# Turning a feed-forward down projection: sign matrix held still, gelu's output moved, two batches a turn

## The chip, the cores and the metric

One core of one Trainium2 chip runs the whole program. The metric is device microseconds of one execution; the kernel before takes 2285.94 us (median of three runs, 2284.62 to 2286.42). PE is the matrix engine, DVE the vector engine, ACT the scalar engine, POOL the GpSimd engine, SP the engine that issues most DMAs.

## The reference

Six blocks follow one another on x of 32 batches of 256 tokens of 128 channels: a feed-forward block with binarised weights, a gated attention unit, the same feed-forward block again, a mixture of experts, a linear attention, the mixture of experts again. The change lies in the feed-forward block, which runs twice:

```python
def _binarize(w):
    alpha = mean(abs(w), axis=1, keepdims=True)
    return alpha * sign(w)
h = gelu(x @ bw1.T + b1)          # 128 channels to 512
out = h @ bw2.T + b2              # 512 to 128: the down projection
x = x + 0.5 * out                 # _L0_ffn_ref(_layernorm(x))
```

Row d of bw2 is a single number alpha[d] times a row of signs, and d is the output's channel.

## The kernel before

x stays in SBUF as 66 tiles of 128 tokens by 128 channels. The six blocks are stages with a barrier between: ffn0, gau1, ffn2, moe3, lin4, moe5, after a short setup. Within a stage every engine has its own program, a fixed order of instructions, and semaphores (`Signal`) join them. `ffn_stage` (line 526) is written for both runs: `first` marks ffn0, `route` marks ffn2.

A turn of the stage is one batch, two tiles. DVE normalises (L262 into `xn`), PE transposes (L690) to bank 4, ACT writes the high part in float32r (L742) and DVE the low part (L605): `parts` holds x as a sum of two float32r numbers. PE's `up` multiplies w1's signs with both parts, 4 chunks of 128 hidden units, eight matmuls of 256 columns (L699). ACT applies gelu to each chunk (L749) into `hT`. PE's `down` (L709) takes `hT` as the stationary operand and `w2T`, the binarised w2 in float32, as the moving one: 2 tiles x 4 chunks = 8 float32 matmuls of 128 columns, each two records in the trace. Tokens come out on partitions, so DVE adds half of them to x (L611), adds the bias (L617 in ffn0; POOL does it ahead in ffn2, L580) and takes the statistics for the next stage's norm (L274).

PE's order in a turn is up(b+1), transpose(b+3), down(b). Beside it, DVE does small pieces of norm work: in ffn0 the statistics of the second half of x, two tiles a batch over sixteen batches, and `norm.piece` (moments, then three Newton steps) for these and for the next stage. POOL computes the position bias of gau1 in ffn0 (`group_bias`, 32 buckets), and a difference of weights.

ffn2 also routes the first four batches of moe3 ahead (`RouteAhead`), by `TURNS_AHEAD` (line 1634): batch n of four begins at batch turn 7 + 5n, and each of its steps stands a number of turns later: norm 0, split 1, choose 2, mask 3, assign 4, first 5 (POOL compares slot numbers, L382, called hot below), hot0 6 and hot1 7 (DVE adds the second choice, L523, and waits for POOL's), sends 8 and 9 (PE, L425).

## Time and profile before

| | us |
|---|---|
| median of three runs | 2285.94 |
| the profiled execution | 2280.57 |
| its span | 2278.7 |
| PE busy in the span | 2170.7 (95%) |
| DVE busy | 1522.8 (67%) |
| ACT busy | 1242.7 (55%) |
| POOL busy | 690.7 (30%) |

Busy time counts an engine's instructions, not its waits. PE's matmuls are pipelined and their ends are modelled, so the spacing of two starts tells more than a duration. The two feed-forward stages are about a tenth of the span.

### The profile page before, as it was taken

The numbers are of one execution on the slowest core, as the hardware profiler recorded it, in microseconds if no ns is written. First come the engines' busy times: TensorE is split into PE (matmuls) and PEld (weight loads), VectorE is DVE, ScalarE is ACT, GpSimd is POOL, SyncE is SP. The second block draws the span as 40 slices with busy tenths as digits, with TensorE's granted clock in tenths as the row PEclk, the third lists the DMA queues.
The fourth block names the chain that finished last, engine by engine and source line by source line (L and its number), as shares of the span: only waits on it lengthen the run. The fifth ranks groups of instructions, "written<-read, shape, count | busy, mean of one in ns | idle before, by whom it ended". The sixth has DMA issues, their size and how long they took to land. (4 is left out here: it accounts for less than half of the span.)

```text
span 2278.7 us, 42519 instructions
## 1 busy us (share of the span) xinstructions
PE 2170.7 (95%) x13706; PEld 1748.3 (77%) x13706; DVE 1522.8 (67%) x4922; ACT 1242.7 (55%) x2504; POOL 690.7 (30%) x724
## 2 busy tenths in 40 slices
PE   5989998999999999899999999999999899999995
PEld 5978888977777777777777777877777777777775
DVE  6867776876777776556565566666666666777664
ACT  4645445754554554465566665666665444545542
POOL 0412222533575655500000000000100344665545
PEclk9999999999999999999999999999999999999998
DMA  8040000000111111200000000000000011111122
GB/s 276 0 176 0 0 0 1 2 10 22 36 41 43 37 38 44 56 7 0 0 0 0 0 0 1 1 1 1 1 1 1 12 28 40 46 51 49 51 55 73
DMA packets 70648, 68.44 MB, mean 30 GB/s; under 512 B 9312, under 2 KB 57952, under 8 KB 70112
## 3 DMA queue, kind: packets, MB, share of 16 engines
q1 hardware_dynamic: 60960, 47.62, 6.6%
q0 software_dynamic: 8192, 16.79, 3.2%
q10 hardware_dynamic: 1344, 2.16, 0.4%
q8 instruction: 76, 1.25, 0.2%
q14 instruction: 76, 0.62, 0.1%
HBM read 32.47 MB, written 34.08 MB: 29 GB/s over the span
## 5 line engine op out<-in xcount | busy, mean ns | idle before, releaser
L2034 ACT ACTIVATE moe_fc<-moe_bank,all_b_fc 128x380 f32<-128x380 f32 (+2 forms) x448 | 245.8, 549 | 277.7 <-PE moe_bank L1964 274.6
L2141 DVE SCALAR_TENSOR_TENSOR moe_act<-moe_bank,all_b_moe_gate,moe_fc 128x380 f32<-128x380 f32 (+2 forms) x448 | 256.7, 576 | 168.3 <-PE moe_bank L1968 101.4
L1980 PEld LDWEIGHTS moe_bank<-all_w_proj,moe_act 128*128 128x128 f32 x2560 | 300.0, 192 | 12.2 <-issue 2.4
L1980 PE MATMUL moe_bank<-all_w_proj,moe_act 128*128 128x128 f32 x2560 | 305.7, 276 | 2.0 <-DVE moe_expert_out L2150 2.0
L1803 POOL DMA_INDIRECT all_landed<-rows_out,all_take_at x256 | 271.7, 1061 | 117.9 <-issue 113.4
L1494 POOL COPY lin_xn_ones<-lin_xn 128x254 f32<-128x254 f32 x32 | 12.7, 398 | 720.7 <-PE lin_bank L1244 720.4
L2041 ACT ACTIVATE moe_act<-moe_act 128x760 f32<-128x760 f32 (+2 forms) x224 | 174.7, 780 | 93.2 <-DVE moe_act L2141 92.7
L1879 POOL TENSOR_SCALAR moe_hot<-all_slot_ids,moe_slot 128x608 fp32r<-128x608 f32 x112 | 203.3, 1824 | 68.3 <-DVE moe_slot L2118 33.7
L1388 ACT ACTIVATE lin_neg<-lin_bank 128x512 f32<-128x512 f32 x256 | 151.7, 592 | 105.5 <-PE lin_bank L1236 61.9
L1286 PEld LDWEIGHTS lin_bank<-lin_kv,lin_qT 128*128 128x128 f32 x1024 | 145.0, 192 | 74.4 <-issue 62.3
L1964 PE MATMUL moe_bank<-gau_rowsT,all_w_fc 128*128 128x380 f32 (+2 forms) x448 | 170.1, 461 | 1.6 <-ACTq L2045 1.6
L1968 PE MATMUL moe_bank<-gau_rowsT,all_w_gate 128*128 128x380 f32 (+2 forms) x448 | 167.6, 456 | 0.8 <-DVE moe_act L2141 0.8
L1392 ACT ACTIVATE lin_neg<-lin_neg 128x512 f32<-128x512 f32 x256 | 161.1, 630 | 7.9
L1416 ACT ACTIVATE lin_gate_tanh<-lin_bank,all_bg_half 128x256 f32<-128x256 f32 x256 | 103.5, 468 | 108.3 <-PE lin_bank L1263 108.2
L1286 PE MATMUL lin_bank<-lin_kv,lin_qT 128*128 128x130 f32 x1024 | 153.5, 277 | 9.1 <-DVE lin_heads L1541 8.7
L749 ACT ACTIVATE ffn_hT<-ffn_bank,all_b,all_alpha 128x256 f32<-128x256 f32 x248 | 119.8, 564 | 57.9 <-PE ffn_bank L699 57.9
L1964 PE MATMUL moe_bank<-moe_rowsT,all_w_fc 128*128 128x380 f32 (+1 forms) x384 | 148.0, 467 | 0.0
L1968 PE MATMUL moe_bank<-moe_rowsT,all_w_gate 128*128 128x380 f32 (+1 forms) x384 | 145.9, 462 | 0.0
L1236 PE MATMUL lin_bank<-all_wk,lin_xT 128*128 128x512 f32 x256 | 131.2, 617 | 2.9 <-ACT lin_xT L1384 1.7
L1556 DVE TENSOR_TENSOR all_x<-lin_bank,all_x 128x256 f32<-128x256 f32 (+1 forms) x32 | 13.6, 425 | 177.2 <-PE lin_bank L1310 177.2
L1310 PE MATMUL lin_bank<-all_wo,lin_gated 128*128 128x128 f32 x1024 | 127.8, 278 | 0.8 <-DVE lin_gated L1550 0.8
L709 PE MATMUL ffn_bank<-all_w2T,ffn_hT 128*128 128x128 f32 x1024 | 125.9, 276 | 1.9 <-DVE all_x L611 1.9
(248 smaller groups left out, 4472.8 us busy)
## 6 DMA issues: line engine op xcount, KB each, us to landing
rows_out<-moe_expert_out SPq DMA_DIRECT2D x96, 128.0 KB
rows_out<-all_zeros SPq DMA_DIRECT2D x1, 9728.0 KB, 28.7
rows_out<-moe_expert_out SPq DMA_DIRECT2D x80, 62.0 KB
all_landed<-rows_out,all_take_at POOLq DMA_INDIRECT x256, 2.7
out<-all_x SPq DMA_DIRECT2D x5, 640.0 KB, 4.5
all_w_fc<-in_w_fc SPq DMA_DIRECT2D x1, 2048.0 KB, 9.8
all_w_gate<-in_w_gate SPq DMA_DIRECT2D x1, 2048.0 KB, 13.6
all_w_proj<-in_w_proj SPq DMA_DIRECT2D x1, 2048.0 KB, 18.1
```

What stands on the lines that cost most here:

```text
L1236: nc.tensor.matmul(bank[j][:, :], xT[:, j // 2 * P:(j // 2 + 1) * P], k.wk[:, j % 2 * HU:(j % 2 + 1) * HU], start=True, stop=True).then_in ...
L1286: last = nc.tensor.matmul(bank[4 + n % 2][:, i * 2 * DH1:(i + 1) * 2 * DH1], qT[:, p, t * P:(t + 1) * P], kv[:, p, :], start=True, stop=True)
L1388: nc.scalar.activation(neg[:, j, :], bank[place][:, :], ACT.Relu, scale=-1.0).then_inc(negs.sem, 1)
L1392: nc.scalar.activation(neg[:, j, :], neg[:, j, :], ACT.Exp, scale=-1.0).then_inc(exps.sem, 1)
L1803: nc.gpsimd.indirect_dma_start(landed[:, b % LANDED, t, h, :], None, k.rows_out, bass.IndirectOffsetOnAxis(take_at[:, i, h:h + 1], 0), bou ...
L1879: nc.gpsimd.tensor_scalar(hot[:, b % 2, t, :], k.slot_ids[:, :], slot[:, b % 2, t, 0:1], None, ALU.is_equal).then_inc(hot_first, 1)
L1964: nc.tensor.matmul(bank[FC + j % 2][:, 0:c.width], k.w_fc[:, e, j * P:(j + 1) * P], rows[c.n][:, e, 0:c.width], start=True, stop=True).the ...
L1968: nc.tensor.matmul(bank[GATE + j % 2][:, 0:c.width], k.w_gate[:, e, j * P:(j + 1) * P], rows[c.n][:, e, 0:c.width], start=True, stop=True) ...
L1980: last = nc.tensor.matmul(bank[OUT][:, j * DIM:(j + 1) * DIM], act_in[:, i % 2, h, j * P:(j + 1) * P], k.w_proj[:, e * MC + h, :], start=( ...
L2034: nc.scalar.activation(fc[:, j, 0:c.width], bank[FC + j % 2][:, 0:c.width], ACT.Identity, bias=k.b_fc[:, e * MC + j:e * MC + j + 1]).then_ ...
L2041: nc.scalar.activation(a, a, ACT.Silu).then_inc(act_sb, 1)
L2141: nc.vector.scalar_tensor_tensor(act_in[:, i % 2, j, 0:c.width], bank[GATE + j % 2][:, 0:c.width], k.b_moe_gate[:, e * MC + j:e * MC + j + ...
```

## The change

The down projection is turned: w2's signs are the stationary operand and gelu's output is the moving one, so the output has channels on partitions. There alpha[d] is a factor per partition. ACT applies it with the bias (`out_columns`, Identity with scale 0.5 alpha and bias 0.5 b2) on the way out of PSUM to `outT`; PE transposes that back into the same bank (`back`), and DVE adds it to x (`add_out`).

A turn is two batches, 512 columns. Of the four chunks of hidden units, two (`SPLIT`) are multiplied in float32r, as a high part, cast by POOL (`gelu_high`), and a low part, subtracted by DVE (`gelu_low`); the other two in float32 (`w2_whole`, `h_whole`). POOL also normalises the second of the two batches. The bias additions of DVE and POOL go. The position bias on POOL is cut into pieces that follow the casts and normalisations of turns 5 to 15; in ffn0 the statistics of x's second half are four tiles per batch turn, at batch turns 0 to 3 and 8 to 11, the norm pieces for them at 4 to 7 and 12 to 15. The routing begins at batch turn 8 instead of 7, and `rowsT` is split in two tensors. The hardware loops of ffn0 are written out.

```diff
-                link(nc.vector.scalar_tensor_tensor(dif[:, 1, :], sgn[:, 1, :], alpha[:, FC:], w2[:, 0, :], ALU.mult, ALU.subtract))
-                nc.vector.tensor_copy(bin_w[:, 0, :], sgn[:, 0, :]).then_inc(bin_ready, 1)
-                nc.vector.tensor_tensor(bin_w[:, 1, :], w2[:, 0, :], dif[:, 1, :], ALU.add).then_inc(bin_ready, 1)
+                for i in range(2):
+                    nc.vector.tensor_copy(bin_w[:, i, :], sgn[:, i, :]).then_inc(bin_ready, 1)
+                nc.vector.tensor_scalar(k.out_scale[:, :], alpha[:, FC:], 0.5, None, ALU.mult).then_inc(prepared, 1)
...
+DUO = 2
+SPLIT = 2
+ON_SCALAR = 0
+TURNS = BATCHES // DUO
+DT = DUO * TILES
+DS = DUO * SEQ
...
+        h_whole = k.sb("h_whole", [P, 2, FC - SPLIT, DS])
+        h_high_of = k.sb("h_high", [P, 2, SPLIT, DS], F32R)
+        h_low_of = k.sb("h_low", [P, SPLIT, DS], F32R)
+        outT = k.zeros if route else k.sb("outT", [P, DS])
...
+                def normalise(p):
+                    pool.wait_ge(xn_ready.sem, xn_ready.at(p))
+                    for t in range(TILES, DT):
+                        last = norm.apply(xn[:, t, :], 0, 0, p * DT + t, engine=nc.gpsimd)
+                    last.then_inc(half_xn.sem, 1)
+                def gelu_high(p):
+                    for c in range(ON_SCALAR, SPLIT):
+                        pool.wait_ge(h_sb.sem, h_sb.at(p, 0, c))
+                        nc.gpsimd.tensor_copy(h_high_of[:, p % 2, c, :], hT[:, c, :]).then_inc(h_high.sem, 1)
+                for p in range(3):
+                    normalise(p)
+                gelu_high(0)
+                for p in range(TURNS):
+                    if p + 1 < TURNS:
+                        gelu_high(p + 1)
+                    if p + 3 < TURNS:
+                        normalise(p + 3)
+                    if first and p >= 5:
+                        group_bias.add(pool, BUCKETS * (p - 5) // (TURNS - 5), BUCKETS * (p - 4) // (TURNS - 5))
+                    if route:
+                        for s in range(DUO):
+                            routing.on_gpsimd(pool, DUO * p + s)
...
+                def low_part(p):
+                    dve.wait_ge(high_sb.sem, high_sb.at(p))
+                    nc.vector.tensor_tensor(parts[:, p % 2, 1, :], bank[ROWS_T][:, :], parts[:, p % 2, 0, :], ALU.subtract).then_inc(xT_sb.sem, 1)
+                def gelu_low(p):
+                    if p:
+                        dve.wait_ge(o_ps.sem, o_ps.at(p - 1))
+                    for c in range(SPLIT):
+                        if c < ON_SCALAR:
+                            dve.wait_ge(h_high_act.sem, h_high_act.at(p))
+                        else:
+                            dve.wait_ge(h_high.sem, h_high.at(p, 0, c - ON_SCALAR))
+                        nc.vector.tensor_tensor(h_low_of[:, c, :], hT[:, c, :], h_high_of[:, p % 2, c, :], ALU.subtract).then_inc(h_low.sem, 1)
+                def add_out(p):
+                    dve.wait_ge(back_ps.sem, back_ps.at(p))
+                    nc.vector.tensor_tensor(rows(p), rows(p), bank[OUT][:, :].rearrange("p (t d) -> p t d", t=DT),
+                                            ALU.add).then_inc(summed.sem, 1)
...
+                def own_norm(b):
+                    if first:
+                        if b < 4 or 8 <= b < 12:
+                            part = b // 8
+                            if b % 8 == 0:
+                                dve.wait_ge(k.x_in[KNOWN + part], 16)
+                            for t in range(2 * TILES):
+                                i = X_PART * (KNOWN + part) + 2 * TILES * (b % 8) + t
+                                last = nc.vector.bn_stats(k.stats[:, i, :], k.x[:, i, :])
+                            if b % 8 == 3:
+                                last.then_inc(late, 1)
+                                dve.wait_ge(late, 2 + part)
+                        elif b < 16:
+                            part, piece = b // 8, b % 8 - 4
+                            lo = X_PART * (KNOWN + part)
+                            norm.piece(dve, chain, lo, X_TILES if part else lo + X_PART, piece)
+                    elif b < PIECES:
+                        norm.piece(dve, chain, AHEAD, X_TILES, b)
...
+                    gelu_low(p)
+                    if p:
+                        add_out(p - 1)
+                    if p + 3 < TURNS:
+                        normalise(p + 3)
+                    if p + 2 < TURNS:
+                        low_part(p + 2)
+                    beside(DUO * p)
+                    if p:
+                        stats(p - 1)
+                    beside(DUO * p + 1)
...
-                def down(b, par):
-                    pe.wait_ge(summed.sem, summed.at(b, -1, 0))
-                    for i in range(2):
-                        pe.wait_ge(h_sb.sem, h_sb.at(b, 0, i))
-                    for t in range(TILES):
-                        for c in range(FC):
-                            last = nc.tensor.matmul(bank[5][:, t * DIM:(t + 1) * DIM], hT[:, par, c, t * P:(t + 1) * P],
-                                                    k.w2T[:, c, :], start=(c == 0), stop=(c == FC - 1))
+                def down(p):
+                    pe.wait_ge(h_sb.sem, h_sb.at(p))
+                    if p:
+                        pe.wait_ge(summed.sem, summed.at(p - 1))
+                    for c in range(SPLIT, FC):
+                        nc.tensor.matmul(bank[OUT][:, :], k.w2_whole[:, c - SPLIT, :], h_whole[:, p % 2, c - SPLIT, :], start=(c == SPLIT), stop=False)
+                    for c in range(SPLIT):
+                        pe.wait_ge(h_low.sem, h_low.at(p, 0, c))
+                        nc.tensor.matmul(bank[OUT][:, :], k.w2T[:, c, :], h_high_of[:, p % 2, c, :], start=False, stop=False)
+                        last = nc.tensor.matmul(bank[OUT][:, :], k.w2T[:, c, :], h_low_of[:, c, :], start=False, stop=(c == SPLIT - 1))
                     last.then_inc(o_ps.sem, 1)
...
+                def back(p):
+                    pe.wait_ge(o_sb.sem, o_sb.at(p))
+                    for t in range(DT):
+                        last = nc.tensor.transpose(bank[OUT][:, t * P:(t + 1) * P], outT[:, t * P:(t + 1) * P], k.ident[:, :])
+                    last.then_inc(back_ps.sem, 1)
...
+                for p in range(TURNS):
+                    if p + 2 < TURNS:
+                        transpose(p + 2)
+                    if p + 1 < TURNS:
+                        up(p + 1, range(2))
+                    if p:
+                        back(p - 1)
+                    if p + 1 < TURNS:
+                        up(p + 1, range(2, FC))
...
+                def out_columns(p):
+                    act.wait_ge(o_ps.sem, o_ps.at(p))
+                    nc.scalar.activation(outT[:, :], bank[OUT][:, :], ACT.Identity, bias=k.b2_half[:, 0:1],
+                                         scale=k.out_scale[:, 0:1]).then_inc(o_sb.sem, 1)
```

PE in ffn2, before: one batch's turn from up to down, and what stands around it (L396 and L402 are the routing's).

```order
L709 MATMUL ffn_bank<-all_w2T,ffn_hT 128x128 x8
L396 MATMUL ffn_bank<-all_ident,ffn_route_xn 128x128 x2
L699 MATMUL ffn_bank<-ffn_x_parts,all_w_signT 128x256 x8
L690 MATMUL ffn_bank<-all_ident,ffn_xn 128x128 x2
L709 MATMUL ffn_bank<-all_w2T,ffn_hT 128x128 x8
L402 MATMUL ffn_bank<-all_w_router,ffn_route_xT 128x8 x2
```

A batch has ten matmuls in up and transpose and eight in down. Now, PE in ffn0, one turn of two batches.

```order
L748 MATMUL ffn_bank<-all_ident,ffn_xn 128x128 x4
L757 MATMUL ffn_bank<-ffn_x_parts,all_w_signT 128x512 x4
L776 MATMUL ffn_bank<-all_ident,ffn_outT 128x128 x4
L757 MATMUL ffn_bank<-ffn_x_parts,all_w_signT 128x512 x4
L766 MATMUL ffn_bank<-ffn_h_whole,all_w_sign_wholeT 128x512 x2
L769 MATMUL ffn_bank<-ffn_h_high,all_w_signT 128x512
L770 MATMUL ffn_bank<-ffn_h_low,all_w_signT 128x512
L769 MATMUL ffn_bank<-ffn_h_high,all_w_signT 128x512
L770 MATMUL ffn_bank<-ffn_h_low,all_w_signT 128x512
```

The two batches' sixteen float32 matmuls of 128 columns have become two of 512 in float32 and four of 512 in float32r, and four transposes (`back`) stand between the halves of up.

POOL in ffn2, around the routing's second batch, before.

```order
L580 TENSOR_TENSOR all_x<-all_x,all_b_half 128x256
L372 CAST ffn_route_parts<-ffn_route_xn 128x256
L374 TENSOR_TENSOR ffn_route_parts<-ffn_route_xn,ffn_route_parts 128x256
L580 TENSOR_TENSOR all_x<-all_x,all_b_half 128x256 x4
L382 TENSOR_SCALAR ffn_route_hot<-all_slot_ids,ffn_route_slot 128x608 x2
```

Between two hots stand bias additions and one split. Now, the same place.

```order
L616 CAST ffn_h_high<-ffn_hT 128x512 x2
L262 TENSOR_SCALAR ffn_xn<-all_x,all_mean,all_rstd 128x128 x2
L616 CAST ffn_h_high<-ffn_hT 128x512 x2
L262 TENSOR_SCALAR ffn_xn<-all_x,all_mean,all_rstd 128x128 x2
L390 TENSOR_SCALAR ffn_route_hot<-all_slot_ids,ffn_route_slot 128x608 x2
L380 CAST ffn_route_parts<-ffn_route_xn 128x256
L382 TENSOR_TENSOR ffn_route_parts<-ffn_route_xn,ffn_route_parts 128x256
```

The hot now stands behind a turn's two casts and two normalisations, and in the same turn of two batches as the split after it.

DVE in ffn2, the same batch, as it is now.

```order
L262 TENSOR_SCALAR ffn_route_xn<-all_x,all_mean,all_rstd 128x128 x2
L668 BN_STATS all_stats<-all_x 128x6 x4
L531 SCALAR_TENSOR_TENSOR ffn_route_hot<-all_slot_ids,ffn_route_slot,ffn_route_hot 128x608
L658 TENSOR_TENSOR ffn_h_low<-ffn_hT,ffn_h_high 128x512 x2
L662 TENSOR_TENSOR all_x<-all_x,ffn_bank 128x512
L262 TENSOR_SCALAR ffn_xn<-all_x,all_mean,all_rstd 128x128 x2
```

DVE's hot0 (L531), which waits for POOL's hot, stands in front of the next turn's gelu_low and add_out.

## Rows read from the trace of the kernel before

**Rows 1.** Busy time by stretch: length, PE, PEld, DVE, ACT, POOL, clock, DMA share, GB/s.

```profile
22.00:132.00 110.00, 99.73 (x832) 96.92 (x832) 88.49 (x312) 71.74 (x161) 26.75 (x71) 1.00 0.26 99
364.00:477.00 113.00, 106.68 (x904) 104.85 (x904) 87.13 (x327) 75.59 (x174) 44.05 (x49) 0.97 0.01 2
```

**Rows 2.** Timeline, first and last of ffn0 and ffn2: start us, us, engine, line.

```profile
22.84 0.60 DVE L262 TENSOR_SCALAR ffn_xn<-all_x,all_mean,all_rstd 128x128 f32<-128x128 f32 x2 [1.22 <-PEq L684]
26.02 2.06 PE L699 MATMUL ffn_bank<-ffn_x_parts,all_w_signT 128*128 128x256 f32 x8
131.46 0.11 DVE L678 TENSOR_SCALAR all_bg_half<-all_bg 128x8 f32<-128x8 f32 x1
364.49 0.60 DVE L262 TENSOR_SCALAR ffn_xn<-all_x,all_mean,all_rstd 128x128 f32<-128x128 f32 x2 [0.81 <-PEq L684]
475.56 0.49 DVE L274 BATCH_NORM_STATS2 all_stats<-all_x 128x6 f32<-128x128 f32 x2
```

**Rows 3.** Timeline of one batch's turn in ffn0.

```profile
102.73 1.20 PE L699 MATMUL ffn_bank<-ffn_x_parts,all_w_signT 128*128 128x256 f32 x8
103.50 1.93 ACT L749 ACTIVATE ffn_hT<-ffn_bank,all_b,all_alpha 128x256 f32<-128x256 f32 x4 [0.77 <-PE ffn_bank L699]
103.77 0.38 PE L690 MATMUL ffn_bank<-all_ident,ffn_xn 128*128 128x128 f32 x2
103.99 1.95 PE L709 MATMUL ffn_bank<-all_w2T,ffn_hT 128*128 128x128 f32 x16
104.01 0.49 DVE L274 BATCH_NORM_STATS2 all_stats<-all_x 128x6 f32<-128x128 f32 x2
105.69 1.20 PE L699 MATMUL ffn_bank<-ffn_x_parts,all_w_signT 128*128 128x256 f32 x8
```

**Rows 4.** Timeline of PE in lin4 (float32) and ffn2 (L425, float32r).

```profile
421.49 0.81 PE L425 MATMUL ffn_bank<-ffn_route_hot,ffn_route_parts 128*128 128x304 f32 x4
422.13 1.11 PE L699 MATMUL ffn_bank<-ffn_x_parts,all_w_signT 128*128 128x256 f32 x8
...
1414.91 1.02 PE L1236 MATMUL lin_bank<-all_wk,lin_xT 128*128 128x512 f32 x2
1415.77 0.50 PE L1286 MATMUL lin_bank<-lin_kv,lin_qT 128*128 128x130 f32 x3
```

**Rows 5.** Groups by line and form: busy us, mean ns, idle before.

```profile
L1528 DVE SCALAR_TENSOR_TENSOR lin_qT<-lin_bank,lin_neg 128x512 f32<-128x512 f32 x128 | 85.3, 687 | 9.2 <-ACT lin_neg L1392 6.8
L1041 POOL TENSOR_SCALAR gau_relu<-gau_sim 128x256 f32<-128x256 f32 x32 | 27.0, 844 | 221.0 <-DVE gau_sim L1103 221.0
L1871 POOL CAST moe_parts<-moe_xn 128x256 fp32r<-128x256 f32 x56 | 22.3, 398 | 249.8 <-DVE moe_xn L262 164.8 <-issue 85.1
L292 POOL TENSOR_SCALAR all_pos_bias<-all_bias_sum 32x32 f32<-32x32 f32 x4 | 1.2, 292 | 0.3
L302 POOL COPY all_wv_less_last_row<-all_ident 128x16 f32<-128x16 f32 x1 | 0.2, 201 | 0.0
```

**Rows 6.** Timeline of ffn0: POOL's position bias, DVE's moments (first and last).

```profile
55.58 0.41 POOL L284 TENSOR_SCALAR all_bias_one<-all_buckets,all_rel 128x32 f32<-128x32 f32 x1
...
84.00 1.40 POOL L292 TENSOR_SCALAR all_pos_bias<-all_bias_sum 32x32 f32<-32x32 f32 x4
84.23 0.17 DVE L227 TENSOR_TENSOR all_mean<-all_stats 128x18 f32<-128x18 f32 x1
...
85.48 0.18 DVE L236 TENSOR_SCALAR all_rstd<-all_var 128x18 uint32<-128x18 uint32 x1
```

**Rows 7.** Timeline, two places where DVE's normalisations meet a POOL instruction.

```profile
85.48 2.39 POOL L300 TENSOR_TENSOR all_wv_less_last_row<-all_wv,ffn_wv_last_row 128x1024 f32<-128x1024 f32 x1
85.69 2.52 DVE L262 TENSOR_SCALAR ffn_xn<-all_x,all_mean,all_rstd 128x128 f32<-128x128 f32 x2
...
410.95 1.05 DVE L262 TENSOR_SCALAR ffn_xn<-all_x,all_mean,all_rstd 128x128 f32<-128x128 f32 x2
411.15 3.73 POOL L382 TENSOR_SCALAR ffn_route_hot<-all_slot_ids,ffn_route_slot 128x608 fp32r<-128x608 f32 x2 [2.17 <-DVE ffn_route_slot L516]
```

More of the change, by code:

```diff
@@ L636, in _, with beside @@
+                def beside(b):
+                    own_norm(b)
+                    next_norm(b)
+                    if route:
+                        routing.read_psum(dve, b)
+                        routing.on_vector(dve, b)
+                for p in range(2):
+                    normalise(p)
+                    low_part(p)
+                normalise(2)
                 if first:
@@ L730, in _ @@
+                if route:
+                    for b in range(BATCHES, routing.last_turn() + 1):
                         routing.on_tensor(pe, b)
+                back(TURNS - 1)
             @block.scalar
             def _(act):
-                act.sem_inc(h_sb.sem, h_sb.credit)
                 if first:
                     act.wait_ge(k.b_in, 32)
-                def high_part(b, lag, par):
-                    act.wait_ge(xT_ps.sem, xT_ps.at(b, lag))
-                    if not (isinstance(b, int) and lag < 2):
-                        act.wait_ge(h_ps.sem, h_ps.at(b, lag - 2))
-                    nc.scalar.copy(parts[:, par, 0, :], bank[4][:, 0:SEQ]).then_inc(high_sb.sem, 1)
@@ L744, in gelu @@
-                def gelu(b, lag, par):
-                    act.wait_ge(o_ps.sem, o_ps.at(b, lag - 2))
-                    for i in range(2):
-                        act.wait_ge(h_ps.sem, h_ps.at(b, lag, i))
-                        for c in (2 * i, 2 * i + 1):
-                            last = nc.scalar.activation(hT[:, par, c, :], bank[2 * par + i][:, (c % 2) * SEQ:(c % 2 + 1) * SEQ],
-                                                        ACT.Gelu, bias=k.b1[:, c:c + 1], scale=k.alpha[:, c:c + 1])
-                        last.then_inc(h_sb.sem, 1)
@@ L753, in _ @@
-                for b in range(2):
-                    high_part(0, b, b % 2)
-                for i in range(2):
-                    act.wait_ge(h_ps.sem, h_ps.at(0, 0, i))
-                    for c in (2 * i, 2 * i + 1):
-                        last = nc.scalar.activation(hT[:, 0, c, :], bank[i][:, (c % 2) * SEQ:(c % 2 + 1) * SEQ],
-                                                    ACT.Gelu, bias=k.b1[:, c:c + 1], scale=k.alpha[:, c:c + 1])
-                    last.then_inc(h_sb.sem, 1)
@@ new lines, in gelu @@
+                def gelu(p):
+                    if p >= 2:
+                        act.wait_ge(o_ps.sem, o_ps.at(p - 2))
+                    for c in range(FC):
+                        act.wait_ge(h_ps.sem, h_ps.at(p, 0, c))
+                        if p and c < SPLIT:
+                            act.wait_ge(h_low.sem, h_low.at(p - 1, 0, c))
+                        nc.scalar.activation(hT[:, c, :] if c < SPLIT else h_whole[:, p % 2, c - SPLIT, :], bank[c][:, :], ACT.Gelu,
+                                             bias=k.b1[:, c:c + 1], scale=k.alpha[:, c:c + 1]).then_inc(h_sb.sem, 1)
+                    if ON_SCALAR:
+                        act.wait_ge(h_sb.sem, h_sb.at(p, 0, 0))
+                        nc.scalar.copy(h_high_of[:, p % 2, 0, :], hT[:, 0, :]).then_inc(h_high_act.sem, 1)
@@ L774, in _ @@
+                for p in range(TURNS):
+                    if p:
+                        out_columns(p - 1)
+                    if p + 2 < TURNS:
+                        high_part(p + 2)
+                    if route:
+                        routing.on_scalar(act, DUO * p)
+                    if p + 1 < TURNS:
+                        gelu(p + 1)
+                    if route:
+                        routing.on_scalar(act, DUO * p + 1)
+                out_columns(TURNS - 1)
                 if route:
```

276 lines of the change are left out of this document (113 added, 163 removed).

## The prediction

> **What bounds the kernel now.** I read the busy times by stretch first, then the timeline of one turn, then the two ends of the stages that the change touches. The profiled execution took 2280.57 us with a span of 2278.7. The two feed-forward stages, ffn0 and ffn2, are 22.84 to 131.57 and 364.49 to 476.05 [rows 2]: 108.7 and 111.6 us, together 220.3. In both, PE is busy for some 100 us and more, at full granted clock but for the start of the second [rows 1]. The reader is to see in the timeline of a turn [rows 3] that PE goes from one group to the next without a hole: eight up matmuls from 102.73, two transposes from 103.77, sixteen records of the down projection from 103.99, the next turn's up from 105.69. So one batch costs 2.96 us and PE sets it. In that turn ACT needs 1.93 us for four gelus, and DVE's instructions are 0.3 to 0.6 us each. POOL has in ffn0 only the position bias, which ends early [rows 6], and in ffn2 one addition a batch and the routing. So the change takes work from the engine that sets the turn, and gives work to two that had room; the question is whether that room lasts.
>
> **The steady turn of two batches.** Per pair PE now spends 2 x 2.96 = 5.92 us. Afterwards, by spacing, it has these to do. The transposes in: four at 0.11 (two took 103.77 to 103.99 [rows 3]) = 0.44; the transposes back, which are new, 0.44 as well. Up: eight float32r matmuls of 512 columns. No row has that width. Eight of 256 take 1.04, 0.13 each [rows 3], so 0.26 is the upper end; a float32 matmul of 512 columns takes 0.86 (1414.91 to 1415.77, two records [rows 4]), and a quarter, 0.215, is the lower. Four of 304 columns took 0.64 [rows 4], between. I take 0.23: 1.84. Down: two float32 matmuls of 512 at 0.86 = 1.72, and four float32r of 512 at 0.23 = 0.92. Before, a pair's down took 2 x 1.70 = 3.40.
>
> Sum 0.44 + 1.84 + 0.44 + 1.72 + 0.92 = 5.36. The chain beside it is as long: the end of down(p-1) reaches ACT in some 0.2, out_columns takes 0.7 (a gelu of 256 columns, also with scale and bias, takes 0.48 with its neighbours, a quarter of 1.93 [rows 3], so 0.5 to 0.97, and part of it is fixed), but back(p-1) stands behind 0.44 of transposes and 0.92 of up, so it starts at 1.36 without waiting and ends at 1.80; add_out (0.69 [rows 5]) ends near 2.75, and PE, through with the second half of up at 2.72, waits 0.05 for it. A turn is 5.41, 0.51 less than now, and sixteen turns give 8.2 a stage if nothing else is late.
>
> **Fill and drain.** The first turn is longer: a normalisation on DVE (0.6 [rows 2]), its other half on POOL (1.4, below), four cold transposes, the cast, low part, and all of it again for the second pair before PE may go to its up (it stands behind transpose(1)): 7.1. Eight cold ups, at double price as the first group of before shows (2.06 for eight, against 1.20 warm [rows 2, 3]), bring 10.8, the last gelu, cast and low part 13.4, and down 2.63: 16.0. Fifteen turns more, the last two at 5.1 since no up is left, make 96.6. The drain is serial: ACT 1.0, back 0.65, add 0.75, statistics 0.9, block end 0.4: 3.7. A stage with nothing in the way would take 100.3.
>
> **What stands in the way in ffn0.** DVE's ordinary turn: two gelu_low, add_out and low_part of 512 columns at 0.62 spacing (0.69 less the 0.07 by which neighbours overlap), two normalisations 0.52, four statistics at 0.205 (0.49 is two [rows 3]): 3.82. That fits in 5.41. But the statistics of x and the norm pieces, which stood spread over sixteen batches, now crowd into turns 0 to 7. Four turns get eight statistics more, 1.64. With some 0.4 of waits they are near 5.85: 4 x 0.45 = 1.8. Two get moments (eight instructions, 84.23 to 85.66 [rows 6], 1.5) and a Newton step (three such instructions, each waiting for the one before, 0.6), 5.9 and waits, 6.5: 2 x 1.1 = 2.2. Two get two Newton steps: 2 x 0.25 = 0.5.
>
> POOL's turn: two casts of 512 columns. 256 take 0.398 and 16 take 0.201 [rows 5], on that line 0.61 each. Two normalisations of 128 columns with two operations: no row; one operation takes 0.29 at 32 and 0.84 at 256 columns [rows 5], and those are my ends; 0.53 lies on their line, and I take 0.7, the nearer to 0.84, for the second operation. At 0.29 the stages would be some 6 us together shorter than I write, at 0.84 some 4 longer. That is 2.6. From turn 5 on it also has the position bias, 0.89 for each of 32 buckets (55.58 to 84.00 [rows 6]), so 2.9 a turn and 2.6 us: 5.2, with waits 5.75, over five turns that are not DVE's already: 5 x 0.35 = 1.8.
>
> Together 6.3: ffn0 takes 100.3 + 6.3 = 106.6, **2.1 less** than now.
>
> **What stands in the way in ffn2.** PE's routing work is the same instructions as before: 106.68 - 99.73 = 7.0 [rows 1], so 107.3. POOL loses the bias additions, but its routing hot, 3.73 for two [rows 7], now shares the queue with casts and normalisations. The order of batch turns 18 and 19, and 28 and 29, is what I look at: POOL's hot and DVE's hot0 fall in the same pair there, where a whole turn lay between them before. POOL comes to hot only after two casts (which start at 3.05 after the last down) and two normalisations, at 6.0; DVE is at hot0 at 6.5 and waits until 7.9, then for POOL's access, and the gelu_low, add_out and normalise behind it are late with PE's down behind them: 2.2, and 0.9 the last time, where little is queued. In the other routing turns POOL's casts start behind hot, or DVE's routing steps meet its fuller turn: 4 x 0.7 = 2.8. Norm pieces 1.2. Together 7.1, bounds 0 and 14: ffn2 takes 107.3 + 7.1 = 114.4, **2.8 more** than now.
>
> Other edits: setup loses one DVE instruction of 512 and has another ACT copy; DVE waits there for x anyway, so nothing. The position bias and the V weights move to POOL's end of ffn0, level with DVE's drain (2.4 for the largest [rows 7]); if POOL is later, up to 2 are lost. The stages after the two are the same instructions.
>
> **Sum.** -2.1 + 2.8 = +0.7. On the median of 2285.94 (5.4 above the profiled execution; I carry that difference over) it is 2286.6; I write 2287.
>
> **A rule weighed.** Casts and DVE's two-input subtractions want the same access. [rows 7] has both answers: a DVE normalisation issued 0.2 after a 2.39 us POOL subtraction ended only with it (2.52 for two, 0.60 free [rows 2]), but two issued around a 1.83 us POOL comparison took 1.05, so only 0.46 was lost. I therefore let a cast hold for most of its 0.61, a hot only for parts, some 0.5 at each end.
> The Trainium skill, page "SBUF — State Buffer", section "Who interferes with whom", says that DVE instructions in a two-port mode, or with two SBUF inputs against a reading POOL instruction, take the shared pair as an exclusive lock for the whole instruction. The subtraction agrees; the comparison does not.
>
> **Rivals.** First, PE's saving stays: the other engines' waits are absorbed: DVE and POOL sums alone (3.82 and 2.6) are far below 5.41, and only PE is at its limit in [rows 1]. Without waits for access ffn0 loses only the crowded turns, half of 6.3, and ffn2 some 1.8 of 7.1: about 220.3 - 103.5 - 109 = -8, 2278. Against: the waits that [rows 7] shows.
> Second, POOL is slower at the two-operation normalisation. If the second operation doubles it, 0.94 each instead of 0.7 (POOL's own end above is 0.84): 0.48 a turn. It decides once POOL's turn with bias is above 5.41, which it then is (2 x 0.61 + 2 x 0.94 + 2.6 = 5.7, and waits, over 6). ffn0 +4, ffn2 +4 (hot0 later still): 2295.
> Third, and slower for certain, POOL holds its access throughout, and DVE waits out each hot and each TENSOR_SCALAR whole: 1.8 rather than 0.5 at up to eight hots in ffn2, and 0.3 more at casts. The four turns with hot go from 6.6 to about 9 by that, +10 in ffn2 and +1.5 in ffn0: 2299, slower. It decides where a DVE instruction meets a hot at its beginning. For it: the subtraction of 2.39. Against: 0.46 behind 1.83.
> The Trainium skill's sentence above, of "SBUF — State Buffer", would give this time.
> Fourth, float32r at 512 columns is at its upper end, 0.26: twelve a turn, 0.36 more, in the half of the turns that PE sets: 16 x 0.36 = 6, 2293. Against it: a float32 record of 512 columns, twice the work a column, takes 0.43. For it: 304 columns took 0.16, as much a column as 0.27 for 512 [rows 4].
>
> **Chances and range.** Forecast (no change, its own range 2282 to 2291): 0.42. Rival 1: 0.22. Rival 2: 0.21. Rival 3: 0.1, rival 4: 0.05. A measurement of this kernel tells 0.2%, 4.6 us, from no change; so faster 0.22, same 0.42, slower 0.36. The range for 8 in 10 runs from rival 1's time to rival 3's with a little at each end: 2277 to 2301.
>
> **What would show it.** The first place is PE between two groups of up matmuls in ffn0's turns 9 to 13: 5.4 to 5.8 apart; 5.9 and more says rival 2. POOL's ffn_h_high cast should last 0.6 and its ffn_xn 0.55 to 0.85. In ffn2 DVE should idle before the hot0 of batch turns 19 and 29, released by POOL. PE's waits should name DVE's add_out (all_x) in crowded turns and ffn_xn of POOL before transposes. The stages should take about 107 and 114. Wrong would be: float32r at 512 columns at more than 0.27 (PE's turn then 5.9 and no gain at all), a turn below 5.3, or time that changes in a later stage.

## The result: 5.3 us slower, 0.2%

| | median us | runs | ratio to before, 95% |
|---|---|---|---|
| before | 2285.48 | 13 | |
| changed | 2290.78 (2286.47 to 2293.03) | 13 | 1.0022 [1.0015, 1.0030] |

The stated range holds the time; it lies 3.8 us above the forecast, and its 5.3 us over before are just outside the 4.6 that the forecast called no change. The two profiled executions are further apart than the medians, 2280.57 and 2288.08, since that of before is one of its shortest. By the first instruction of each stage (the changed kernel's rows answer to [rows 2]; the last stage runs to the end of the span):

```profile
22.18 0.60 DVE L262 TENSOR_SCALAR ffn_xn<-all_x,all_mean,all_rstd 128x128 f32<-128x128 f32 x2 [0.94 <-PEq L129]
133.88 0.60 DVE L262 TENSOR_SCALAR gau_z<-all_x,all_mean,all_rstd 128x128 f32<-128x128 f32 x2 [1.00 <-PEq L926]
361.52 0.60 DVE L262 TENSOR_SCALAR ffn_xn<-all_x,all_mean,all_rstd 128x128 f32<-128x128 f32 x2 [0.54 <-DVE all_stats L274]
479.18 0.21 ACT L2121 ACTIVATE moe_tanh_gap_ahead<-all_gap_ahead 128x8 f32<-128x8 f32 x1 [2.42 <-PEq L588]
```

| us | before | before, a second profile | changed |
|---|---|---|---|
| ffn0 | 109.7 | 109.3 | 111.7 |
| gau1 | 231.9 | 232.3 | 227.6 |
| ffn2 | 112.3 | 112.3 | 117.7 |
| moe3 | 479.4 | 479.6 | 481.3 |
| lin4 | 821.0 | 821.0 | 823.3 |
| moe5 | 501.5 | 502.6 | 502.4 |

The two stages cost 7.3 us more, and gau1, moe3 and lin4, whose instructions are the same, moved by -4.3, +1.9 and +2.2 (moe5 by +0.9 against the one profile of before and by -0.2 against the other). Inside a turn the profile looks much as forecast. The timeline of one turn of ffn0 after the change, which answers to [rows 3]:

```profile
99.10 0.66 PE L748 MATMUL ffn_bank<-all_ident,ffn_xn 128*128 128x128 f32 x4 [0.17 <-POOL ffn_xn L262]
99.51 1.17 PE L757 MATMUL ffn_bank<-ffn_x_parts,all_w_signT 128*128 128x512 f32 x4
100.52 0.60 PE L776 MATMUL ffn_bank<-all_ident,ffn_outT 128*128 128x128 f32 x4
100.88 1.19 PE L757 MATMUL ffn_bank<-ffn_x_parts,all_w_signT 128*128 128x512 f32 x4
101.99 1.96 PE L766 MATMUL ffn_bank<-ffn_h_whole,all_w_sign_wholeT 128*128 128x512 f32 x4
103.61 1.60 POOL L262 TENSOR_SCALAR ffn_xn<-all_x,all_mean,all_rstd 128x128 f32<-128x128 f32 x2
104.02 0.40 PE L770 MATMUL ffn_bank<-ffn_h_low,all_w_signT 128*128 128x512 f32 x1
104.26 0.39 PE L769 MATMUL ffn_bank<-ffn_h_high,all_w_signT 128*128 128x512 f32 x1
104.49 0.40 PE L770 MATMUL ffn_bank<-ffn_h_low,all_w_signT 128*128 128x512 f32 x1
105.27 0.66 PE L748 MATMUL ffn_bank<-all_ident,ffn_xn 128*128 128x128 f32 x4 [0.38 <-POOL ffn_xn L262]
```

float32r of 512 columns starts every 0.235 us (0.23 forecast), a turn that nothing delays takes 5.55, and here PE waits at its transposes for POOL's normalisation, as the prediction named it. The granted clock is another matter. Windows of the changed kernel (from and to, length, busy us of PE, PEld, DVE, ACT, POOL, then the clock as a share of full speed, DMA):

```profile
122.00:124.70 2.70, 0.96 (x7) 0.47 (x5) 2.42 (x5) 0.78 (x1) 2.24 (x6) 1.00 0.00 0
124.70:129.30 4.60, 4.53 (x8) 2.12 (x8) 3.08 (x13) 0.03 (x1) 3.92 (x9) 0.63 0.00 2
466.00:469.70 3.70, 0.94 (x6) 0.42 (x4) 3.63 (x7) 0.78 (x1) 1.92 (x2) 1.00 0.01 2
469.70:474.20 4.50, 4.46 (x9) 2.26 (x10) 3.21 (x14) 0.00 (x0) 0.00 (x0) 0.62 0.00 0
479.00:490.00 11.00, 9.43 (x36) 6.66 (x37) 4.76 (x21) 6.24 (x12) 1.79 (x4) 0.84 0.01 1
```

In the last turn PE has no up left. It is busy for 0.96 of 2.70 us (0.94 of 3.70 in ffn2), waiting for ACT's out_columns and then DVE's add_out, and the granted clock falls from 1.0 to 0.5 (2.4 to 1.2 GHz) behind that: the last down takes 4.4 us in both stages, where others take 2.7. The clock falls again at the start of the mixture of experts, where it was 1.0 before:

```profile
476.63:488.00 11.37, 9.43 (x42) 6.46 (x43) 6.21 (x28) 7.04 (x15) 2.41 (x6) 1.00 0.01 1
```

In gau1 the opposite happened. Windows of before, then of the changed kernel:

```profile
139.10:142.50 3.40, 1.48 (x10) 1.06 (x9) 2.01 (x8) 1.68 (x4) 1.47 (x2) 0.99 1.04 387
142.50:145.90 3.40, 3.40 (x9) 2.69 (x9) 1.54 (x5) 1.34 (x3) 0.00 (x0) 0.50 1.03 386
```

```profile
139.00:146.00 7.00, 5.08 (x29) 4.10 (x28) 4.70 (x14) 3.71 (x9) 1.47 (x2) 1.00 1.05 409
```

Before, the clock fell a second time, behind a stretch in which PE was busy for 1.48 of 3.40 us; after the change it didn't. Both kernels also have a fall at the stage's start, and after the change that one began earlier, at the end of ffn0. Together gau1 ran at 0.5 for 9.9 us before and for 4.9 after. At half the clock 5.0 us less are worth 2.5 (an estimate), most of the 2.8 that it gained in its first 30 us (the rest of the 4.3 builds up in small steps over its first 160 us, and stays unexplained).

Each timed run also has a mean granted clock. Its median is 0.984 over the changed kernel's 13 runs and 0.987 over the 94 runs of before beside the experiments. Among the runs of either kernel a clock lower by 0.001 goes with 0.9 to 1.7 us more, so 0.003 go with some 3 to 5 us (an estimate): most of the difference.

### The profile page after: what moved, and what is told of

Same layout as the page of the kernel before. It is cut to its first block and busy times, and to the rows that moved or that the text cites. A ratio compares the mean times of both kernels' runs of the same rounds, so it can differ in the third digit from the quotient of the medians.

```text
span 2286.2 us, 40200 instructions
## 1 busy us (share of the span) xinstructions
PE 2164.8 (95%) x12810; PEld 1678.4 (73%) x12810; DVE 1521.6 (67%) x4826; ACT 1234.1 (54%) x2377; POOL 768.1 (34%) x820
## 5 line engine op out<-in xcount | busy, mean ns | idle before, releaser
L1569 POOL COPY lin_xn_ones<-lin_xn 128x254 f32<-128x254 f32 x32 | 12.8, 401 | 722.9 <-PE lin_bank L1319 722.5
L2039 PE MATMUL moe_bank<-moe_rowsT,all_w_fc 128*128 128x380 f32 (+1 forms) x576 | 226.0, 474 | 0.0
L2043 PE MATMUL moe_bank<-moe_rowsT,all_w_gate 128*128 128x380 f32 (+1 forms) x576 | 222.9, 469 | 0.0
L2043 PEld LDWEIGHTS moe_bank<-moe_rowsT,all_w_gate 128*128 128x128 f32 x576 | 109.2, 190 | 66.7 <-DVE moe_act L2216 0.9
L2225 DVE TENSOR_TENSOR moe_expert_out<-moe_bank,all_b_proj 128x384 f32<-128x384 f32 (+1 forms) x112 | 60.0, 536 | 100.6 <-PE moe_bank L2055 99.2
L1338 PE MATMUL lin_bank<-lin_xT,all_wg 128*128 128x256 f32 x512 | 126.5, 380 | 0.3 <-DVE lin_qT L1603 0.3
L1330 PE MATMUL lin_bank<-lin_xT,all_wq 128*128 128x256 f32 x512 | 125.8, 379 | 0.0
```

The lines of the kernel that those rows point to most:

```text
L2039: nc.tensor.matmul(bank[FC + j % 2][:, 0:c.width], k.w_fc[:, e, j * P:(j + 1) * P], rows[c.n][:, e, 0:c.width], start=True, stop=True).the ...
L2043: nc.tensor.matmul(bank[GATE + j % 2][:, 0:c.width], k.w_gate[:, e, j * P:(j + 1) * P], rows[c.n][:, e, 0:c.width], start=True, stop=True) ...
```

## Experiments

All times are medians; the kernel before ran beside each (2284.4 to 2285.2).

**The kernel before once more.**

> The kernel before once more, for a second profile of it. Between the two profiles on hand the stages that the change doesn't touch also differ: the gated attention's stage takes 231.9 us before and 227.6 after, and everything from the mixture of experts on 1801.9 and 1807.0. Theory: both are what two executions differ by; this profile then shows the later stages at 1803 to 1808 and the attention's stage between 227 and 232. Rival: the change itself makes the later stages 5 us longer and the attention's 4 us shorter; then this one shows 1802 and 232 again.

2281.03 in its profiled run. The rival holds: moe3 and lin4 are 479.6 and 821.0 again, gau1 232.3. In all kernels made from the changed one lin4 took between 821.0 and 823.9, with the granted clock at its start low for a shorter or longer time. So what the change does to later stages, it does through where PE's clock happens to fall in them. The traces bear this out: in all fourteen profiles lin4 took 821.0 to 821.1 where the clock was at 0.5 for 10.2 us of it, 821.9 to 822.9 for 13.7 and 823.0 to 823.9 for 17.1; moe3 took 479.4 to 479.7 without a fall and 481.0 to 481.7 with one.

**The routing's second choice one batch turn later.**

```diff
-"first": 5, "hot0": 6, "hot1": 7, "send0": 8, "land0": 9, "send1": 9, "land1": 10}
+"first": 5, "hot0": 7, "hot1": 8, "send0": 9, "land0": 10, "send1": 10, "land1": 11}
```

> Only the routing's table is changed: DVE's second choice (hot0) and all behind it come one batch turn later, so that POOL's comparison and DVE's hot0 no longer fall in the same turn of two batches. Theory: the two waits of 1.7 us of DVE for POOL's hot, in turns 9 and 14, go; turn 9 (7.9 us from down to down) and the turn with the other come to some 6.5; the last send comes a little later: 2 to 3 us less, 2288. Rival: it is POOL's queue (casts and normalisations behind two hots of 3.6 to 4.1 us) and the held access that make these turns long, and not DVE's wait; then the turns keep their 7 to 8 us and the time is 2290 to 2292.

2292.75, 1.0028 [1.0019, 1.0037]: not faster. In the changed kernel the wait is there in turn 9 as predicted: POOL's hot, DVE's hot0 and PE's down behind DVE's addition. (In turn 14, where the expectation has it too, the trace shows no such wait of DVE.)

```profile
432.10 3.60 POOL L390 TENSOR_SCALAR ffn_route_hot<-all_slot_ids,ffn_route_slot 128x608 fp32r<-128x608 f32 x2
433.95 1.35 DVE L531 SCALAR_TENSOR_TENSOR ffn_route_hot<-all_slot_ids,ffn_route_slot,ffn_route_hot 128x608 fp32r<-128x608 f32 x1 [1.73 <-POOL ffn_route_hot L390]
437.45 1.96 PE L766 MATMUL ffn_bank<-ffn_h_whole,all_w_sign_wholeT 128*128 128x512 f32 x4 [1.73 <-DVE all_x L662]
```

With the later hot0 turn 9 takes 5.99 instead of 7.92 us and turn 14 5.31 instead of 6.34, but turn 10 takes 8.46 instead of 7.00 and turn 8 7.03 instead of 6.24:

```profile
437.75 1.73 POOL L616 CAST ffn_h_high<-ffn_hT 128x512 fp32r<-128x512 f32 x2
439.48 1.58 POOL L262 TENSOR_SCALAR ffn_xn<-all_x,all_mean,all_rstd 128x128 f32<-128x128 f32 x2
441.11 0.65 PE L748 MATMUL ffn_bank<-all_ident,ffn_xn 128*128 128x128 f32 x4 [2.04 <-POOL ffn_xn L262]
```

POOL's casts and normalisations stand behind two hots and a split, and PE's transposes behind those. Turns 7 to 14 take 53.4 us together instead of 54.1: most of the wait moved to the next queue, as the rival (POOL's queue) has it.

**30 of 32 buckets of the position bias left out.**

```diff
-if first and p >= 5:
-    group_bias.add(pool, BUCKETS * (p - 5) // (TURNS - 5), BUCKETS * (p - 4) // (TURNS - 5))
+if first and p in (5, TURNS - 1):
+    group_bias.add(pool, p // (TURNS - 1), p // (TURNS - 1) + 1)
```

> 30 of the 32 buckets of the position bias are left out (so the attention's bias is not the reference's), which takes 2.6 us of POOL's time out of each of ffn0's turns 5 to 15. Theory: POOL's queue sets ffn0's turns 8 to 12 (30.2 us from down to down for the five, instead of 27.0 at PE's 5.4), since PE's transposes wait for POOL's half of the normalisations: the five come to 27.0 to 28.0 and the stage loses 2.5 to 3 us: 2288. Rival: DVE, with its waits, is as late as POOL, or PE sets the turn anyway; then the five keep some 29.5 to 30 and the time stays within 0.7 us.

2290.76, no change. But ffn0's turns 8 to 12 are 5.58, 5.58, 5.55, 5.55, 5.58: 27.8 us together instead of 30.2, as the theory said. Most of it was given back in the last turn:

```profile
119.90 2.35 POOL L308 TENSOR_TENSOR all_wv_less_last_row<-all_wv,ffn_wv_last_row 128x1024 f32<-128x1024 f32 x1
119.93 3.48 DVE L658 TENSOR_TENSOR ffn_h_low<-ffn_hT,ffn_h_high 128x512 fp32r<-128x512 f32 x2
124.15 3.46 PE L766 MATMUL ffn_bank<-ffn_h_whole,all_w_sign_wholeT 128*128 128x512 f32 x4 [2.79 <-DVE all_x L662]
```

POOL, earlier now, comes to the weights difference while DVE has the last gelu_low to do (3.48 us for two, 1.29 free), PE waits 2.79, and its four records take 3.46 instead of 1.96, at the low clock.

**No normalisation on POOL.**

```diff
-                    if p + 3 < TURNS:
-                        normalise(p + 3)
...
-                    for t in range(TILES):
+                    for t in range(DT):
                         last = norm.apply(xn[:, t, :], 0, 0, p * DT + t)
```

> POOL's half of the normalisations goes to DVE, in both stages and all turns: POOL has 1.6 us a turn less, DVE 0.52 more. Theory: POOL's queue makes the long turns (hots of 3.6 to 4.1 with casts and normalisations behind them, for which PE's transposes and DVE's subtractions wait; the bias in ffn0's turns 8 to 12): the four long turns of ffn2 come from 7.0 to 7.9 down to some 6.3, 4 to 5 us together, ffn0's turns 8 to 12 from 30.2 to 28, and the fill is 1.5 shorter in each stage; against it DVE's crowded turns 0 to 6 of ffn0 are 0.5 longer each: 2282 to 2286. Rival: it is DVE that is late in those turns, by its own load and by waiting for POOL's access behind the hot; then the long turns stay or grow by 0.5 each: 2290 to 2295.

2288.74, 1.0017 [1.0008, 1.0026], not told apart from the changed kernel's 1.0022; 2282 to 2286 had been expected. The long turns 7, 9 and 12 of ffn2 are 6.97, 7.02 and 6.84 (7.66, 7.92 and 7.29), but turn 10 is 8.24 (7.00), at full clock; there PE idles for 1.22 us and its sends start 0.1 behind the end of an addition of the second choice on DVE (441.47 to 442.30). The four long turns lost 0.8 us together, not 4 to 5. The fills are 2.0 and 3.6 us shorter, ffn0's turns 8 to 12 5.55 to 5.58; but its turns 1 to 7 are 6.0 to 6.9 (they were 5.6 to 6.6), and ffn2's turns 0 to 3 went from 5.5 to 5.6 up to 5.9 to 6.3, with PE behind DVE:

```profile
392.92 1.71 DVE L262 TENSOR_SCALAR ffn_xn<-all_x,all_mean,all_rstd 128x128 f32<-128x128 f32 x4
393.14 1.95 PE L753 MATMUL ffn_bank<-ffn_h_whole,all_w_sign_wholeT 128*128 128x512 f32 x4 [0.68 <-DVE all_x L650]
```

So POOL bounds the turns with a hot or the bias, DVE the others as soon as it gets more.

**The last down in a bank of its own.** The transposes' bank is free by then.

```diff
+        def out(p):
+            return bank[OUT if p < TURNS - 1 else ROWS_T]
...
-                    if p:
+                    if 0 < p < TURNS - 1:
                         pe.wait_ge(summed.sem, summed.at(p - 1))
...
+                    if p == TURNS - 1:
+                        back(p - 1)
```

> Only the last turn of both feed-forward stages is changed: its down projection goes to the PSUM bank of the transposes, which is free by then, so it waits neither for the addition of the turn before nor for its transposes back. Theory: in the changed kernel PE stands idle for some 2 us in the last turn, its granted clock then falls to 0.5 for 3.4 us and the last down takes 4.5 instead of 2.7 us; without the hole the clock stays at 1.0 there, the last down ends some 4 us earlier in ffn0 and 3 to 4 in ffn2 (where the routing's last sends then set the end): 2283 to 2285 us. Rival: the clock falls at the end of the stage whatever PE does; then only the hole of some 2 us a stage goes, and the drop shows in the last down all the same: 2287 to 2288.

2289.05, 1.0016 [1.0007, 1.0025]: 3.8 us over before instead of 5.3, with overlapping intervals, and above what theory and rival had (2283 to 2288). Over the last down the clock stays at 1.0, as the theory said, and it ends 3.7 us earlier. ffn0 isn't shorter all the same:

```profile
126.38 0.66 PE L782 MATMUL ffn_bank<-all_ident,ffn_outT 128*128 128x128 f32 x4 [0.87 <-ACT ffn_outT L833]
127.81 2.35 POOL L308 TENSOR_TENSOR all_wv_less_last_row<-all_wv,ffn_wv_last_row 128x1024 f32<-128x1024 f32 x1
127.87 2.42 DVE L242 SCALAR_TENSOR_TENSOR all_norm_tmp<-all_rstd 128x112 f32<-128x112 f32 x1
130.94 0.69 DVE L666 TENSOR_TENSOR all_x<-all_x,ffn_bank 128x512 f32<-128x512 f32 x1
```

The last transposes are done at 127.0; the addition comes at 130.94, behind a Newton step that waits out POOL's difference (2.42 us, 0.27 at its fellows). PE then stands idle for longer, and gau1 takes 230.7 instead of 227.6, at 0.5 of the clock for 11.4 us instead of 4.9. ffn2 with nothing of the kind is 3.3 us shorter (114.35).

**The same, and the weights difference in turn 4.** Its call at the end goes.

```diff
+                    if first and p == 4:
+                        weights_less_last_row(k, pool, last_row, wv1_done)
```

> The last down into its own bank, as in the run with only the last turn changed, and POOL's weights difference (2.35 us) in ffn0's turn 4 instead of at the end. Theory: in that run the last down of ffn0 ended 4 us earlier, but DVE's last Newton step stood behind POOL's difference (2.42 us instead of 0.28), with the last addition to x behind it, so that the stage was as long as before; with the difference gone from there ffn0 is 2 to 2.4 us shorter (111.7 to 109.4) and PE's hole in front of the attention is shorter by as much: 2285 to 2287. Rival: the wait moves to turn 4, where a normalisation or subtraction of DVE waits 2 us and the turn is longer by that: 2289.

2288.48, 1.0019 [1.0009, 1.0028]: mostly the rival. The end is 2.2 us shorter (12.3 from the start of the second-last down to gau1, against 14.4), and turn 4 is 6.97 instead of 5.68, where a gelu_low now waits:

```profile
62.21 2.38 POOL L308 TENSOR_TENSOR all_wv_less_last_row<-all_wv,ffn_wv_last_row 128x1024 f32<-128x1024 f32 x1
63.02 2.72 DVE L663 TENSOR_TENSOR ffn_h_low<-ffn_hT,ffn_h_high 128x512 fp32r<-128x512 f32 x2
```

**PE kept busy where it only waits.**

```diff
+                def keep(n):
+                    pe.wait_ge(h_sb.sem, h_sb.at(TURNS - 1))
+                    for i in range(n):
+                        nc.tensor.matmul(bank[0][:, :], k.ident[:, :], h_whole[:, TURNS % 2, 0, :], start=True, stop=True)
...
+                    if p == TURNS - 1:
+                        keep(1)
                     if p:
                         back(p - 1)
+                    if p == TURNS - 1:
+                        keep(1 if first else 2)
...
+                if first:
+                    keep(1)
                 back(TURNS - 1)
+                keep(2)
```

> The changed kernel, and PE multiplies into a free PSUM bank where it only waits at the end of both stages: one float32 matmul of 512 columns (0.86 us) before the last turn's transposes back, one (two in ffn2) between these and the last down, one in ffn0 behind the last down, and two behind the last transposes. No other engine's work and no wait is changed, and nothing reads the result. Theory: a good part of what the change loses is the granted clock, which falls to 0.5 behind PE's holes at the ends of the stages (for 3.4 us in each last down, 6.8 us at the start of the attention, 3.4 us at the start of the mixture of experts); without the holes the last down takes 2.7 instead of 4.5 us and the next stage starts at 1.0 or falls later and for less: 4 to 6 us less, 2285 to 2287. Rival: the clock falls at these places whatever PE does in them: 2290 to 2292.

2286.42, 1.0005 [0.9996, 1.0014], whose interval ends below that of the changed kernel: 2.0 us over before instead of 5.3, by matmuls that compute nothing of use, and at a median clock of 0.987 as before. Windows of it over ffn0's last down, a place within ffn2, the waits in ffn2's last turn and the start of moe3:

```profile
126.60:129.90 3.30, 3.29 (x10) 1.81 (x10) 3.06 (x13) 0.20 (x1) 2.62 (x9) 1.00 0.01 2
441.00:444.60 3.60, 3.60 (x7) 1.74 (x6) 3.48 (x18) 1.06 (x2) 2.95 (x4) 0.53 0.00 0
471.60:475.00 3.40, 3.17 (x11) 1.54 (x11) 3.29 (x8) 0.07 (x1) 0.89 (x1) 1.00 0.01 2
483.00:493.00 10.00, 8.61 (x40) 5.78 (x39) 6.00 (x26) 6.55 (x13) 1.52 (x3) 1.00 0.00 0
```

The clock stays up over the last downs and at the start of moe3; the last downs take 2.7 again and moe3 479.7. The profile is of the longest of its 11 runs (2289.51) and shows only a part of the gain: in gau1 the clock is at 0.5 for 6.8 us instead of 4.9, and gau1 takes 229.3. The second row shows what an execution can add by itself: behind turn 9's hole of 1.72 us the clock fell this time, and turn 10 took 8.44. Five profiles have this hole (1.70 to 1.73); in two the clock fell behind it (turn 10 8.44 and 8.50), in three it didn't (7.00 to 7.03).

**Versions that put these together.** The first has the last down's bank, the difference in turn 4, the bias in turns 8 to 15, spare matmuls behind the last downs, and POOL normalising only pairs 3 to 10 of ffn0. The third has the difference in turn 3, DVE's constants in turn 9, one more spare matmul at ffn0's end and:

```diff
+        on_pool = [4, 5, 6, 7, 8, 9, 10] if first else [3, 4, 5, 6, 7, 8, 11]
...
-                    if p + 3 < TURNS:
+                    if p + 3 in on_pool:
                         normalise(p + 3)
```

> Several together, for a version that beats both kernels: the last down into its own bank, the weights difference in turn 4, PE's spare matmuls behind the last downs, POOL normalising only pairs 3 to 10 of ffn0 and DVE all else, the position bias over turns 8 to 15. Theory: the fill is 1.5 shorter a stage, ffn0's turns 8 to 12 come to 5.6, ffn2's long turns lose 1 us or more each, the ends 2 to 4 each, the clock less of its falls: ffn0 about 105, ffn2 with the start of the next stage 8 us less than in the changed kernel: 2276 to 2281. Rival: what is taken from one queue comes back as a wait in another, and the clock falls at the stages' ends all the same: 2284 to 2288.

2281.44, 0.9985 [0.9976, 0.9994]: its interval lies below that of before and of the changed kernel.

> The version that beat the kernel before, with six edits: in ffn2 POOL normalises pairs 3 to 8 and 11 (not those of the turns at and behind a hot), in ffn0 pairs 4 to 10; the weights difference in turn 3 instead of 4; DVE's three constants in turn 9 instead of the end; one more spare matmul at ffn0's end; and the routing's hot0 and all behind it one batch turn later, as in the run of the table alone. Theory: there the later hot0 gave nothing since PE then waited 2 us for POOL's normalisation in the turn after, and it was POOL's queue that cost; where DVE normalises in these turns it takes the two waits of 1.7 us away; ffn2's ordinary turns come back from 5.9 to 6.6 to 5.5 to 6.1 and ffn0 loses 1 to 2 more: 2276 to 2279. Rival: DVE is the bound of the routing's turns by now and the later hot0 only moves its work: 2280 to 2282.

2280.75, 0.9983 [0.9972, 0.9994]. Against the next version, which lacks it, the later hot0 again gives nothing: turns 8 to 10 are 7.04, 6.60 and 7.34 (6.32, 7.60 and 7.54 without it), and from the second-last down to the stage's end, where the last sends come a batch turn later and the clock falls behind PE's wait for them, it takes 17.1 us instead of 12.8.

> The same version without the later hot0. Theory: 1 to 3 us more than with it, 2278 to 2281, since DVE still waits for POOL's hot in turns 9 and 14 and PE for DVE's addition behind it, where the granted clock can fall. Rival: no difference, or less than with it, if DVE's sum sets these turns.

2274.86, 0.9954 [0.9937, 0.9971], **10 us less than before, where the change as it was took 5 more**, and less than its theory had (2278 to 2281). ffn0 takes 104.9, ffn2 111.5.

> The fastest version without its spare matmuls of PE at the ends of the two stages. Theory: in the changed kernel such matmuls alone were worth some 4 us, through the granted clock behind the stages' ends; here the ends' holes are shorter, so that 2 to 4 us of the version's 10 come from them: 2277 to 2279. Rival: the waits that went are the whole of the gain, and the time stays within 1 us of the version with them, 2275.

2278.76, 0.9973 [0.9964, 0.9982]: by the medians the spare matmuls are worth 3.6 us here, but the two intervals overlap. The median clock is 0.985 instead of 0.989. The end of ffn2 and the start of moe3, from 8.7 us before moe3's first instruction to 7.3 behind it, without them, then with them:

```profile
462.00:478.00 16.00, 11.24 (x38) 7.76 (x37) 8.29 (x27) 4.13 (x9) 1.79 (x4) 0.68 0.00 1
```

```profile
459.70:475.70 16.00, 12.44 (x52) 7.60 (x50) 10.40 (x38) 6.12 (x11) 2.36 (x5) 1.00 0.00 1
```

**The kernel before with two spare matmuls.** They stand behind ffn0's last down.

```diff
+                if first:
+                    for i in range(2):
+                        nc.tensor.matmul(bank[0][:, :], k.ident[:, :], k.w2T[:, :, :].rearrange("p c d -> p (c d)"), start=True, stop=True)
```

> The kernel before, with two spare float32 matmuls of 512 columns (0.86 us each) on PE behind ffn0's last down, where it waits 3.6 us for the attention's first norm. Theory: its attention starts at a granted clock of 0.5 for 6.8 us and falls again for 3.4; a shorter hole makes these falls shorter, 1 to 4 us less, 2281 to 2284, so that a part of what the fastest version gains is open to the kernel before as well. Rival: the barrier's hole is enough by itself for the fall: no change, 2284 to 2286.

2282.71, 0.9988 [0.9979, 0.9997]: 2 us are open to the kernel before as well. Its profile shows the theory at work, but not the whole gain: in gau1 the clock is at 0.5 for 6.8 us instead of 9.9 and 10.2, and gau1 takes 231.3 instead of 231.9 and 232.3, but ffn0 takes 111.3, with a fall within it that the profiles of before don't have. Compared bare with bare, the repaired change gains 0.27%.

## Why the prediction was right, and where it was not

- **PE's turn**: 5.41 worked out, 5.55 measured. float32r at 0.235 came within 0.005, so rival 4 (0.26) is out; the rest is mostly some 0.1 in front of each down.
- **Crowded turns 0 to 7 of ffn0**: 47.7 worked out (four at 5.85, two at 6.5, two at 5.66), 47.5 measured. Here the sum by DVE's instructions was right, turn for turn.
- **Turns 8 to 12**: 28.8 worked out, 30.2 measured. The turns took 5.7 to 6.4 each, where the prediction had 5.4 to 5.8 and took 5.9 and more as rival 2's sign. POOL's two-operation normalisation is 0.80, between the 0.7 taken and rival 2's 0.94, and the cast 0.62 as on the line; the run without the bias shows that POOL's queue is the cause. That queue had one more wait, which the prediction priced only for DVE: once in each of these turns a bias instruction of POOL that starts within DVE's two gelu_low ends only behind them, after 0.92 to 1.33 us instead of 0.40.

```profile
98.98 1.29 DVE L658 TENSOR_TENSOR ffn_h_low<-ffn_hT,ffn_h_high 128x512 fp32r<-128x512 f32 x2 [1.18 <-PE ffn_bank L770]
99.15 1.32 POOL L289 TENSOR_SCALAR all_bias_one<-all_buckets,all_rel 128x32 f32<-128x32 f32 x1
```

- **hot0**: in turn 9 DVE waited 1.73 for POOL (1.4 worked out, from 6.5 to 7.9) and PE 1.73 behind that (2.2 forecast). In turn 14 PE waited 1.93 (0.9 forecast), but DVE's hot0 had no wait there: two small instructions of DVE's moments took 0.65 and 0.71 instead of 0.2 beside POOL's hot. Right in place, but taking hot0 out of turn 9 gained little: the run with the later hot0 shows POOL's queue behind it.
- **The access.** Half right: a subtraction of POOL blocked DVE outright in three more places (2.42 for 0.27, 3.48 and 2.72 for 1.29). Beside a hot DVE lost only 0.5: hot0 took 1.35 instead of 0.83 and ended at 435.30, when POOL's second hot still ran until 435.70. So the third rival, with the whole hot held, is out. The Trainium skill, "SBUF — State Buffer", "Who interferes with whom", agrees with the subtractions by its rule of the exclusive lock. By the same rule hot0, with two inputs in SBUF, would have waited out the hot; there it doesn't agree, and the measurement decides.
- **Fill and drain, the step that failed.** 16.0 and 3.7 worked out; 16.8 and 3.8 measured in ffn0, 17.2 and 4.3 in ffn2. ffn0's serial drain was right to 0.1, but the prediction took the last down at full clock and counted "the last two at 5.1 since no up is left" as a gain. With no up left PE stands idle in the last turn, and the last down costs 1.8 more in each stage by its clock; the run with spare matmuls in that hole, where it takes 2.7, shows that the hole is the cause. Of the fills' 0.8 and 1.2, 0.8 and 0.6 were lost before the first up, 0.4 of it by POOL (1.6 for two normalisations instead of 1.4, twice); in ffn2 the clock was still at 0.5 when the third pair came, unlike in ffn0 (first row):

```profile
33.99 0.66 PE L748 MATMUL ffn_bank<-all_ident,ffn_xn 128*128 128x128 f32 x4 [0.49 <-POOL ffn_xn L262]
373.15 1.12 PE L748 MATMUL ffn_bank<-all_ident,ffn_xn 128*128 128x128 f32 x4 [0.18 <-POOL ffn_xn L262]
```

- **"The stages after the two are the same instructions."** True, and they moved by -4.3, +1.9 and +2.2, which the prediction itself had named as what would make it wrong. The forecast had no term for the clock behind a hole, though [rows 1] showed 0.97 in ffn2.
- **Rival 1**, PE's saving stays: its time (2278) was reached only where the waits were taken out (0.9954, or 0.9973 without spare matmuls); as the change stood, its saving went into waits for POOL and DVE, a longer drain and the clock.

In sum, from first instruction to last, ffn0 came out at 110.7 instead of 106.6 (last down 1.8, turns 8 to 12 1.4, fill 0.8) and ffn2 at 116.9 instead of 114.4 (last down 1.8, fill 1.2, drain 0.6, the turns 1.0 less). The two stages are 6.6 us over the forecast, and that the time came within 3.8 of it is luck: in the profiles gau1 gave back 4.3, about as much as moe3 and lin4 took. The range was wide enough to hold the time without that.

## What to carry to other kernels

Where a change takes work from PE, count what PE does in the turns in which it has nothing left: here the holes in the last turns (PE busy for 0.96 of 2.70 us) cost themselves and 1.8 us more in the next down, at half the clock. A wait taken out of one queue shows up in the queue behind it, so look for the engine whose instructions stand behind the long one (here POOL's normalisations behind hot), not for the one that waits. Spare matmuls into a free bank are a cheap test of what the clock costs.
